# Scattering expert results into the output and adding the rest by accumulating DMAs

## The reference, cut to what matters

```
xn  = layernorm(x)                                   # 2048 tokens x 256
att = (A[:, None, :] * Q(xn)) @ W_out + b_out + xn   # one vector A per batch
y   = sum over experts e: scatter_add(rows of e, weight * ffn_e(xn[rows of e]))   # 16 experts, at most 128 rows each
shared = silu(xn @ sw_gate) * (xn @ sw_up) @ sw_down
out = x + att + y + shared
```

## Time and profile before

| | |
|---|---|
| median of 3 runs | 177.37 us |
| the profiled execution, device time | 177.02 us |
| its span in the trace | 175.1 us |
| TensorE busy | 161.0 us (92%) |
| VectorE busy | 107.0 us (61%) |
| GpSimd busy | 92.4 us (53%) |
| ScalarE busy | 75.9 us (43%) |
| granted TensorE clock, mean | 0.997 of full speed |

### The profile page before, as it was taken

The page is one execution under the profiler, slowest core; times in us unless marked ns, Lnnn a source line. Parts: engine busy times, 40 slices in busy tenths (PEclk is TensorE's granted clock), DMA queues, the critical chain, the costliest instruction groups (busy, mean ns, idle before and its releaser), DMA issues.

```text
span 175.1 us, 3144 instructions
## 1 busy us (share of the span) xinstructions
PE 161.0 (92%) x1021; PEld 132.8 (76%) x1021; DVE 107.0 (61%) x321; ACT 75.9 (43%) x226; POOL 92.4 (53%) x111
## 2 busy tenths in 40 slices
PE   7887698999899899999999998999999999999960
PEld 5555697899786678977778967867887886699950
DVE  1866997879943344788656875762754313274590
ACT  3123446967458784545645534354222425410000
POOL 5446689800225936798449855963633333032940
PEclk9999999999999999999999999999999999999998
DMA  4999979030794216574476564635755220228667
GB/s 141 353 394 343 539 248 349 10 120 4 180 258 137 67 34 169 153 169 122 122 184 161 161 152 99 159 86 140 188 105 115 34 29 1 30 30 269 217 221 255
DMA packets 25363, 28.66 MB, mean 164 GB/s; under 512 B 4098, under 2 KB 24163, under 8 KB 25316
## 3 DMA queue, kind: packets, MB, share of 16 engines
q1 hardware_dynamic: 20898, 23.03, 40.7%
q0 software_dynamic: 3072, 4.33, 14.1%
q10 hardware_dynamic: 1378, 1.12, 2.1%
HBM read 21.77 MB, written 8.79 MB: 175 GB/s over the span
## 4 chain that ended last, share of the span: by engine, by line
PE 39%; DMA 21%; DVE 18%; POOL 8%; issue 7%; ACT 3%; SPq 1%; DVEq 0%; POOLq 0%; ACTq 0%
DMA ysum<-eo,idx 10%; PE bank L1098 8%; PE bank L236 7%; PE bank L238 5%; PE bank L237 5%; DMA xg<-rows,idx 4%; PE bank L1109 4%; DMA x_all<-ysum 4%; POOL ysum L387 3%; PE bank L1108 3%; DMA x_all<-in_x 3%; DVE st L614 2%; DVE xt_all L644 2%; PE bank L1087 2%; PE bank L1134 1%
## 5 line engine op out<-in xcount | busy, mean ns | idle before, releaser
L387 POOL DMA_INDIRECT ysum<-eo,idx x16 | 28.4, 1773 | 28.6 <-DMA ysum<-eo,idx 15.0
L236 PE MATMUL bank<-wkvr_s,xt_all 128*128 128x256 f32 (+1 forms) x96 | 29.1, 304 | 4.0 <-DVE xt_all L644 3.5
L379 POOL DMA_INDIRECT xg<-rows,idx x16 | 20.3, 1267 | 15.9 <-ACT eo L553 8.4
L238 PE MATMUL bank<-wkvr_s,xt_all 128*128 128x256 f32 (+1 forms) x96 | 27.3, 284 | 0.0
L237 PE MATMUL bank<-wkvr_s,xt_all 128*128 128x256 f32 (+1 forms) x96 | 27.2, 283 | 0.0
L1098 PE MATMUL bank<-xgt,wgu 128*128 128x128 f32 (+1 forms) x192 | 24.0, 275 | 0.6 <-ACT xgt L538 0.6
L1098 PEld LDWEIGHTS bank<-xgt,wgu 128*128 128x128 f32 (+1 forms) x192 | 22.4, 187 | 0.8 <-issue 0.8
L236 PEld LDWEIGHTS bank<-wkvr_s,xt_all 128*128 128x128 f32 x96 | 18.1, 189 | 5.4 <-DVE xt_all L644 4.4
L236 PE MATMUL bank<-xt_all,sw_s 128*128 128x512 f32 (+1 forms) x48 | 19.9, 416 | 0.0
L238 PE MATMUL bank<-xt_all,sw_s 128*128 128x512 f32 (+1 forms) x48 | 19.0, 395 | 0.0
L237 PE MATMUL bank<-xt_all,sw_s 128*128 128x512 f32 (+1 forms) x48 | 18.9, 395 | 0.0
(11 more groups left out here) (157 smaller groups left out, 355.0 us busy)
## 6 DMA issues: line engine op xcount, KB each, us to landing
wgu<-in_w_gu SPq DMA_DIRECT2D x16, 368.0 KB, 2.9
rows<-xn_all SPq DMA_DIRECT2D x4, 512.0 KB, 5.2
wdn<-in_w_dn SPq DMA_DIRECT2D x16, 128.0 KB, 3.1
x_all<-ysum SPq DMA_DIRECT2D x4, 512.0 KB, 6.6
x_all<-in_x SPq DMA_DIRECT2D x3, 512.0 KB, 7.4
trg<-in_trig SPq DMA_DIRECT2D x1, 1024.0 KB, 7.9
out<-xn_all ACTq DMA_DIRECT2D x4, 256.0 KB, 2.2
out<-xn_all SPq DMA_DIRECT2D x4, 256.0 KB, 2.7
```

The source lines that it names most:

```text
L236: nc.tensor.matmul(dst, lt_hi, r_hi, start=start, stop=False)
L238: return nc.tensor.matmul(dst, lt_lo, r_hi, start=False, stop=stop)
L379: nc.gpsimd.indirect_dma_start(out=xg[:, e % G, :], out_offset=None, in_=rows, in_offset=bass.IndirectOffsetOnAxis(ap=idx[:, e:e + 1], axi ...
L387: nc.gpsimd.indirect_dma_start(out=ysum, out_offset=bass.IndirectOffsetOnAxis(ap=idx[:, e:e + 1], axis=0), in_=eo[:, e % G, :], in_offset= ...
```

## The change: what it does

`ysum` is gone. The kernel's output tensor is filled with x by the copy that filled `ysum`, and the scatters accumulate into it. It has no spare rows, so scatters get a bounds check that drops rows beyond the last token, and the DMA that zeroed the spare rows goes. At the end nothing is loaded back and nothing is added from it: when the last scatter has landed, GpSimd issues eight DMAs of two tiles each, in the order 0 to 15, that add `sh` onto the output. VectorE's mixes from tile 8 on no longer wait for GpSimd, and the stores from ScalarE's and SyncE's queues are gone.

```diff
-        ysum = nc.dram_tensor("ysum", (TOKENS + CAP, D), F32, kind="Internal").ap()
...
-            sp.dma_start(ysum[0:TOKENS, :], x_rows).then_inc(ysum_set, 16)
+            sp.dma_start(out_rows, x_rows).then_inc(out_set, 16)
...
-            sp.dma_start(ysum[TOKENS:TOKENS + CAP, :], zero[:, 0:D]).then_inc(pads_saved, 16)
...
-            sp.wait_ge(acc_done, TILES)
-            sp.wait_ge(scat_done, 16 * E)
-            for g in (2, 3, 0, 1):
-                sp.dma_start(yin[:, g * G:(g + 1) * G, :], ysum_v[:, g * G:(g + 1) * G, :]).then_inc(y_in[g], 16)
-
-            for t in range(0, 2 * G, 2):
-                sp.wait_ge(ot_dve, min(t + 2, 5))
-                if t >= G:
-                    sp.wait_ge(ot_pool, (9, 11)[t // 2 - 2])
-                sp.dma_start(out_v[:, t:t + 2, :], sh[:, t:t + 2, :]).then_inc(out_sent[t // 2], 16)
             for sent in out_sent:
                 sp.wait_ge(sent, 16)
...
-                nc.gpsimd.indirect_dma_start(out=ysum, out_offset=bass.IndirectOffsetOnAxis(ap=idx[:, e:e + 1], axis=0),
-                                             in_=eo[:, e % G, :], in_offset=None, compute_op=ALU.add).then_inc(scat_done, 16)
+                nc.gpsimd.indirect_dma_start(out=out_rows, out_offset=bass.IndirectOffsetOnAxis(ap=idx[:, e:e + 1], axis=0),
+                                             in_=eo[:, e % G, :], in_offset=None, bounds_check=TOKENS - 1, oob_is_err=False,
+                                             compute_op=ALU.add).then_inc(scat_done, 16)
...
-            def add_y(t):
-                pool.wait_ge(y_in[t // G], 16)
-                nc.gpsimd.tensor_tensor(sh[:, t, :], sh[:, t, :], yin[:, t, :], ALU.add).then_inc(ot_pool, 1)
...
+            pool.wait_ge(scat_done, 16 * E)
+            for t in range(0, TILES, 2):
+                pool.wait_ge(half_done, t + 2)
+                nc.gpsimd.dma_start(out=out_v[:, t:t + 2, :], in_=sh[:, t:t + 2, :], accum_op=ALU.add).then_inc(out_sent[t // 2], 16)
...
-            for t in range(2 * G, TILES, 2):
-                act.wait_ge(half_done, t + 2)
-                act.dma_start(out_v[:, t:t + 2, :], sh[:, t:t + 2, :]).then_inc(out_sent[t // 2], 16)
...
             def mix(t):
                 dve.wait_ge(kept, 2 * (t // G) + 2)
-                if t >= 2 * G:
-                    dve.wait_ge(ot_pool, t - 2 * G + 1)
                 dve.wait_ge(att_done, t + 1)
...
-            for t in range(2 * G, 3 * G):
+            for t in range(2 * G, TILES):
                 mix(t)
-            add_y(0)
-            mix(3 * G)
...
-            add_y(4)
-            mix(3 * G + 3)
```

More of the change, by code:

```diff
@@ L123, in layer @@
         x_all = sb("x_all", [P, TILES, D])
-        k_all = yin = x_all
+        k_all = x_all
         xn_all = sb("xn_all", [P, TILES, XW])
@@ L186, in layer @@
             sem(n) for n in ("id_in", "cst_in", "gb_in", "vr_in", "kq_in", "sw_in", "gr_in", "mix_in", "trg_in"))
-        zero_set, ones_set, table_set, pads_saved, ysum_set, xn_saved, wd_saved = (
-            sem(n) for n in ("zero_set", "ones_set", "table_set", "pads_saved", "ysum_set", "xn_saved", "wd_saved"))
+        zero_set, ones_set, table_set, pads_saved, out_set, xn_saved, wd_saved = (
+            sem(n) for n in ("zero_set", "ones_set", "table_set", "pads_saved", "out_set", "xn_saved", "wd_saved"))
         ew_in, gath = sems("ew_in", G), sems("gath", G)
@@ L210, in layer @@
             sem(n) for n in ("red_done", "cs_done", "comb_done", "acol_done", "aw_done", "m_done", "m_hi", "m_lo"))
-        s2_done, att_done, half_done, ot_pool, ot_dve = (
-            sem(n) for n in ("s2_done", "att_done", "half_done", "ot_pool", "ot_dve"))
-        y_in, out_sent = sems("y_in", GROUPS), sems("out_sent", 2 * GROUPS)
+        s2_done, att_done, half_done = (sem(n) for n in ("s2_done", "att_done", "half_done"))
+        out_sent = sems("out_sent", 2 * GROUPS)
         x_v = x.rearrange("b (t p) d -> p (b t) d", p=P)
@@ L217, in layer @@
         out_v = out.rearrange("b (t p) d -> p (b t) d", p=P)
+        out_rows = out.rearrange("b s d -> (b s) d")
         rows_v = rows.rearrange("(t p) d -> p t d", p=P)
-        ysum_v = ysum.rearrange("(t p) d -> p t d", p=P)
         w_v = w_in.rearrange("(c p) n -> p c n", p=P)
@@ L398, in _ @@
             pool.wait_ge(xn_saved, 16 * GROUPS)
-            pool.wait_ge(pads_saved, 32)
+            pool.wait_ge(pads_saved, 16)
             pool.wait_ge(idx_done, 1)
@@ L404, in _ @@
             query_weights()
-            pool.wait_ge(ysum_set, 16)
+            pool.wait_ge(out_set, 16)
             for e in range(E):
@@ L413, in _ @@
             scatter(E - 1)
-            def add_y(t):
-                pool.wait_ge(y_in[t // G], 16)
-                nc.gpsimd.tensor_tensor(sh[:, t, :], sh[:, t, :], yin[:, t, :], ALU.add).then_inc(ot_pool, 1)
-            pool.wait_ge(kept, 6)
-            for t in range(2 * G, 3 * G):
[L421 to L427, removed]
+            pool.wait_ge(scat_done, 16 * E)
+            for t in range(0, TILES, 2):
+                pool.wait_ge(half_done, t + 2)
+                nc.gpsimd.dma_start(out=out_v[:, t:t + 2, :], in_=sh[:, t:t + 2, :], accum_op=ALU.add).then_inc(out_sent[t // 2], 16)
         @block.scalar
@@ L856, in _ @@
             dve.wait_ge(table_done, GROUPS)
-            dve.wait_ge(pads_saved, 32)
+            dve.wait_ge(pads_saved, 16)
             dve.wait_ge(zero_set, 2)
```

## The result

The changed kernel took 180.38 us in the median of four runs (180.12 to 180.91), against 177.19 for the kernel before beside it. The ratio is **1.020, interval 1.016 to 1.024**: slower, by just about the 2% that a measurement here can tell, with the interval on both sides of it. The forecast was 179.5 us, most likely no change. Some executions of every kernel run slower, at a lower granted clock; ratios here compare only the others, while the traces of e3_plain_hw and e4_half_half are of such slower executions, so of these two traces the tail counts and not the time.

The account below looks back on a forecast made before the run. TensorE bounds the kernel before; afterwards GpSimd's eight DMAs end generating at 174.0, + 0.45 + 1.9 + 0.4 + 0.7 = 177.45 us span, giving 179.4 or 179.7 as time, stated as 179.5. Range 175.8 to 187.5.

Parts of the forecast that it names:

- The removal, 1.0 us: Tail: without reload and adds, VectorE's last mix ends at 169.67 instead of 170.68, mixes 0.72 us apart.
- Generation, 1.85 us: GpSimd's time to generate one accumulating DMA of 256 rows, the middle of 1.07 and 2.63.
- My 2.63: Generation in us if the accumulation's 0.52 is work per row: 1.59 + 2 x 0.52.
- the rival that I gave 0.30: Generation grows with rows, so GpSimd's run of eight DMAs binds: 181.5 to 190 us, chance 0.30.
- The transfers: Data of one two-tile accumulating DMA: 1.9 us, counted once after the last generation and 0.45 until packets begin.
- my pitch of 2.15 us: Time between starts of GpSimd's output DMAs: 1.85 us generation plus 0.30 between two DMAs.
- the DMA engines are the bound: Rival: eight accumulating transfers of 2.3 us each occupy the DMA engines from 159.1; about 180.4 us, chance 0.09.
- the sign I had named for it: Last generation's end to span end much longer than 3.45 us with full engines would mean the transfers.
- The closing, 0.4 + 0.7 us: End of kernel: 0.4 us from last packets to landing, then 0.7 to the end of the span.
- The bounds check, taken at 0 for the time: Scatters: check costs 0; upper end 0.3 us each, 1.2 over four in the loop, 0.3 at the last.
- The fill, the spare rows and the loop at nothing: Filling the output instead of `ysum`, dropping the spare rows' zeroing, and the loop's scatters were costed at 0.
- My span of 177.45: Forecast end of the traced span in us, 2.35 more than the 175.1 before.

Follow-up runs that it names:

- e3_plain_hw: Changed kernel, its eight accumulating GpSimd DMAs replaced by plain overwriting stores from the hardware queues; 174.18 us, ratio 0.983 to the kernel before.
- e4_half_half: Changed kernel, but tiles 8 to 15 read back, added by GpSimd and stored plainly from ScalarE's queue; 175.61 us, ratio 0.990 to the kernel before.
- e10_second_half_adds: Changed kernel, but tiles 0 to 7 stored by plain overwriting SyncE DMAs, only tiles 8 to 15 accumulated; 180.26 us, ratio 1.018 to the kernel before.
- e11_no_bounds_check: Changed kernel without the bounds check on its scatters; 180.79 us, ratio 1.014 to the kernel before.
- e5_spare_dma: Changed kernel with the DMA that zeroed the spare rows put back, to a tensor nobody reads; 180.15 us, ratio 1.016 to the kernel before.
- e6_front_and_loop: Kernel before, tail kept, with bounds check on scatters and without spare rows or their zeroing DMA; 177.87 us, ratio 1.004 to the kernel before.
- e8_four_tiles: Changed kernel with four accumulating DMAs of four tiles (512 rows) instead of eight of two; 180.96 us in a single execution.
- e2_plain_gpsimd: Changed kernel, its eight GpSimd DMAs overwriting instead of accumulating; 177.50 us, ratio 1.000 to the kernel before.

## Why the prediction was right or wrong, point by point

**The removal, 1.0 us: right.** From the start of the last result to the end of the last mix it was 170.68 - 152.33 = 18.35 us before and 170.60 - 153.29 = 17.31 after. The pace of 0.72 us between mixes held.

**Generation, 1.85 us: wrong, it is 1.19.** The step that failed is the reading of the earlier trace rows. I took the 0.52 us between scatter and gather as work per row. It belongs to the accumulation as such (1.19 against 0.71 for the same 256 direct rows), and rows cost almost nothing (1.19 to 1.26 from 256 to 512). My 2.63 was also added up wrongly: 1.59 holds the 0.52 once already, so doubling it gives 2.11. The rule of the Trainium skill, page "DMA: Bandwidth & Descriptors", section on the anatomy of a software-generated DMA, that many descriptors come before the incremental cost shows, was right here. So the rival that I gave 0.30, GpSimd's queue as the bound, was dead.

**The transfers: the right size, the wrong place in the sum.** I took 1.9 us for two tiles; the second half, 1 MB, took from 168.3 to 175.9, 1.9 each. But I counted one of them behind the last generation, since at my pitch of 2.15 us the engines would have kept up. With the pairs ready every 1.44 us and 1.9 us to move each, they don't, and four queue up from the moment tile 9 is mixed. The rival "the DMA engines are the bound" (0.09, about 180.4 us) is the mechanism that happened, and the sign I had named for it came: from the last generation's end to the end of the span it took 6.2 us instead of 3.45, with the engines full. Its detail was off too: I let it begin with the first DMA, while e10_second_half_adds and e11_no_bounds_check show that only the last four count. The first four have drained by 167.8, just before the next data.

**The closing, 0.4 + 0.7 us: mis-sized.** From the last packets (175.9) to the end of the span it took 2.4 us. Most of the difference is GpSimd's drain: it ended 1.6 us after SyncE had seen the landing, and 1.4 to 1.9 us after it in every trace whose last DMA is GpSimd's, accumulating or not. In e4_half_half, whose last stores are ScalarE's, the span closed 0.4 after the landing.

**The bounds check, taken at 0 for the time: right for the end, not for the scatter.** It costs each scatter 0.5 us between its wait and its start (0.27 before, 0.78 after), and the last one 0.3 more of generation. All of that is covered in both tails.

**The fill, the spare rows and the loop at nothing: not contradicted.** e5_spare_dma and e6_front_and_loop show no effect that can be told, and the loop took 98.4 us in both traces.

**How the errors add up.** My span of 177.45 from the last result at 152.33 is a tail of 25.1 us, and 25.0 were measured. This agreement is luck of signs. The last generation ended 2.9 us earlier than I said (172.1 less the front's 0.96, against 174.0). From there to the last packets it took 3.8 us instead of 2.35, and the closing 2.4 instead of 1.1, which is 2.75 us back. The rest of the miss, 178.3 against 177.45, is the front's 0.96 us, a clock dip that the kernel before also shows. The range was also very wide, and its lower end should by its own sum be 176.0, not 175.8.

Against that rival I had leaned on the best slices of the scatter. The Trainium skill, page "Collectives: The Full Stack", section on the bandwidth ceiling, says of a collective's reduce that it reads two sources and so runs at half the copy's rate. Here 138 GB/s (1.05 MB in 7.6 us) is 0.4 of the plain 350, and my average over the scatter's packets (115 GB/s) was nearer than its best slices (174); only the 512 KB pieces of e8_four_tiles came to half, some 180 GB/s.

## What to carry to other kernels

An accumulating DMA trades an engine's add for a transfer that held the DMA engines 2.5 times as long here (about twice with 512 KB in each); it is worth having only where other work still covers it. Find out which bytes become ready last and cost the transfer for those alone, from the moment the first of them is ready. Keep the last store of a kernel off GpSimd, and before a difference of 1 us is laid to an edit, profile the unchanged kernel more than once and count from a landmark behind the part that varies.

## What the runs showed of the hardware that I had not expected

- Generation on GpSimd is nearly flat in rows (at least 0.94, 1.19 and 1.26 us for 128, 256 and 512 rows), and accumulation adds 0.48 us (0.71 without it).
- Accumulating DMAs of 256 KB moved 138 to 150 GB/s with all engines full, those of 512 KB some 180.
- A plain GpSimd DMA of two tiles left in 64 data packets of four rows each (320 packets for four DMAs, 64 of them small), an accumulating one in 256 of one row (1088 for four, 64 small). That alone doesn't make it slow: the plain stores of the earlier trace rows, from the hardware queues, also left in packets of about 1 KB (816 for 0.79 MB) and ran at some 340 GB/s. A plain GpSimd DMA in packets of 1 KB wasn't tried.
- GpSimd's closing drain ends 1.6 us after its last DMA is seen landed (178.1 against 176.5; 176.0 against 174.4 in e2_plain_gpsimd).
- A bounds check on an indirect DMA puts a register move between its wait and its start, 0.5 us in all.
- TensorE's clock halved for a few microseconds somewhere in the first 60 us in 12 of 14 traces, one of the three of the kernel before included. In the trace after it fell to 0.50 at 17 us, behind a gap of about a microsecond in TensorE's work, but the trace of before has the same gap without a fall. What decides it stays open.
